# The fullest expert taken first, its first two thirds beside the last block's routing

## The chip, the cores and the metric

The kernel runs on one core of a Trainium2 chip. The metric is the device time of one execution in microseconds (us): the median of three runs, and beside it one execution taken with the hardware profiler.

## The reference

One transformer layer over 4096 tokens of width 256, on one sequence. Attention has 16 heads of width 16, LoRA terms on its three projections, an ALiBi bias and a causal mask. A mixture of 8 experts follows, two per token, each expert with a capacity of 1076 rows. Both halves add their input and end in a layer norm.

```python
x = _layernorm(x + attention(x))           # softmax(q k / 4 + slope (i - j), causal) v, then Wp
probs = softmax(x @ Wg)                    # 8 experts
topv, topi = top_k(probs, 2); gates = topv / sum(topv)
pos = (place of the token among those of its expert, in order of tokens); keep = pos < 1076
dest = where(keep, expert * 1076 + pos, dropped)
h = gelu(expert_in @ W1[e] + b1[e])        # 256 -> 1024, each expert
y = h @ W2[e] + b2[e]                      # 1024 -> 256
x = _layernorm(x + sum over the two choices of y[dest] * gate * keep)
```

## The kernel before

The five engines (and SyncE, which issues most DMAs) each run a list of instructions written out by hand, with waits on semaphores; nothing reorders them. There are two blocks of code, with a barrier of all engines between them: `attend` and `experts`.

`attend` runs 411 turns. It takes the queries in 8 blocks of 512 and, beside the attention of later blocks, routes the earlier ones: `Router` multiplies a block's attention by Wp, normalizes it, chooses two experts per row (`choose`), counts rows per expert (`pe_count` on TensorE, `places` on VectorE), and GpSimd scatters the rows into `slots_x` in DRAM, 1076 rows for each expert. `PIECE_AT`, `SCATTER_AT` and similar tables say in which turn each piece runs. Blocks 0 to 6 are routed there; the last scatter of block 6 is in turn 379, and `FLAG_TURN` is 382.

The last block (7) can only be routed when all of attention is done, so that is the start of `experts`, in class `Last`. VectorE scales the attention rows (`scale_last`), TensorE multiplies them by Wp (L2083), VectorE normalizes and chooses (`vector`), TensorE counts (L1870), ScalarE applies the norm (L2198), GpSimd issues eight scatters (L2034). Meanwhile SyncE loads the fp32 weights of experts 0 and 1 and the constants (`Last.sync`), and TensorE runs 80 matmuls whose result nobody reads (`warm`, L2093). When the last scatter has landed, SyncE loads the rows of experts 0 and 1 (L2334 to L2336).

Each expert then has 9 tiles of 128 rows (the ninth has 52), in three groups `SB` of three tiles. TensorE transposes the tiles (`transpose`, L2398), runs 8 `up`s for each group (6 matmuls each, L2410), and a `down` for each tile (24 matmuls, L2429). Matmuls are done in three products of bf16 halves: a high half (cast) and a low half (the difference). ScalarE does the gelu (`hidden`, L2477), VectorE the two halves of its result (`split`, L2529 and L2531) and the output (`out`), ScalarE and GpSimd the two halves of the weights (`weights_high` L2257, `weights_low` L2263), and GpSimd adds the weighted rows to the result in DRAM (L2366). PSUM holds four results of `up` (`ps_h`), so `up` number q waits for the gelu of number q - 4. All experts compute all their 9 tiles, however full they are. `Combine` ends the kernel with the second layer norm.

A register is loaded from SBUF in one place before: `flag_of` (L883), by each engine in turn 382, followed by two register instructions and a jump over a path that isn't taken.

## Time and profile before

| | us |
|---|---|
| median of 3 runs | 1240.04 |
| lowest, highest | 1238.25, 1240.32 |
| the profiled execution, its own time | 1237.03 |
| its span, first to last instruction | 1235.0 |
| TensorE busy | 1157.4 |
| ScalarE busy | 904.3 |
| VectorE busy | 637.3 |
| GpSimd busy | 351.2 |

The profile gives the busy time of each engine, a timeline of instructions with what ended the idle time before them, and busy times by window. Attention fills the span to 781 us, the last block's routing goes to 819, the eight experts to 1199, and the last layer norm to the end. A row with "x8" is eight instructions, its time the stretch that they fill. SPq and ACTq are the issues of DMAs. PEld is TensorE's loading of weights, which overlaps its matmuls.

### The profile page before, as it was taken

Reading aid. Unit: us, or ns where it says so; the run is one execution under the profiler, and the core shown is the slowest. Engines: PE = TensorE matmul, PEld = TensorE weight load, DVE = VectorE, ACT = ScalarE, POOL = GpSimd, SP = SyncE. Lnnn points to the kernel's source line nnn. Section 1 sums busy time; section 2 is a strip of 40 time slices with the busy share of each in tenths; the row PEclk is TensorE's granted clock in tenths of the full one; section 3 lists DMA queues with packets and bytes.
Section 4 is the critical chain, followed back from the end, with each engine's and each line's share of the span. In section 5 each row is a group of like instructions: output and inputs, shape, how many; then the busy total and the mean of one; then the engine's idle time right before and its main releaser. Section 6 shows DMA issues by size and latency. Waiting matters only on the chain. (4 is left out here: it accounts for less than half of the span.)

```text
span 1235.0 us, 24778 instructions
## 1 busy us (share of the span) xinstructions
PE 1157.4 (94%) x8880; PEld 507.9 (41%) x8880; DVE 637.3 (52%) x1802; ACT 904.3 (73%) x1181; POOL 351.2 (28%) x391
## 2 busy tenths in 40 slices
PE   9999999999999999999999989699999999999980
PEld 4322222222222222222222111277777777787770
DVE  5644343132366335734353203548767767767747
ACT  3889999999998999999999989344434435535314
POOL 5421111101123112232122220033453453552440
PEclk9999999999999999999999999799999999999995
DMA  6743421322321331213120100543443523430226
GB/s 194 169 109 81 95 67 59 81 87 73 82 76 52 111 86 42 73 64 101 45 74 31 47 14 26 180 141 84 115 74 81 129 37 101 122 35 11 28 23 272
DMA packets 84100, 104.10 MB, mean 84 GB/s; under 512 B 15416, under 2 KB 69309, under 8 KB 83985
## 3 DMA queue, kind: packets, MB, share of 16 engines
q1 hardware_dynamic: 66520, 76.80, 22.0%
q0 software_dynamic: 15968, 24.12, 9.3%
q10 hardware_dynamic: 1496, 1.68, 0.5%
q8 instruction: 68, 1.11, 0.4%
q14 instruction: 48, 0.39, 0.1%
HBM read 56.88 MB, written 47.96 MB: 85 GB/s over the span
## 5 line engine op out<-in xcount | busy, mean ns | idle before, releaser
L1491 ACT ACTIVATE prob<-ps_s 128x1024 f32<-128x1024 f32 (+4 forms) x841 | 706.1, 999 | 46.6 <-PE ps_s L1380 44.7
L1397 PE MATMUL ps_o<-prob,v_aug 128*17 128x512 f32 (+3 forms) x3236 | 423.5, 570 | 3.5 <-DVE acc L1575 2.8
L1380 PE MATMUL ps_s<-qop,kop 51*128 51x512 f16 (+3 forms) x1618 | 260.4, 369 | 18.6 <-ACT prob L1491 7.2
L1380 PEld LDWEIGHTS ps_s<-qop,kop 51*128 51x128 f16 x1618 | 62.5, 93 | 386.1 <-ACT prob L1491 366.8
L2429 PE MATMUL ps_y<-w2s,hs 128*128 128x256 bf16 (+1 forms) x1728 | 189.1, 273 | 1.2 <-DVE yb L2515 1.2
L2410 PE MATMUL ps_h<-xs,w1s 128*128 128x384 bf16 (+1 forms) x1152 | 179.9, 316 | 5.2 <-ACT hid L2477 4.4
L2477 ACT ACTIVATE hid<-ps_h,b 128x384 f32<-128x384 f32 (+1 forms) x192 | 105.0, 559 | 108.7 <-PE ps_h L2410 83.7
L1575 DVE COPY acc<-ps_o 32x512 f32<-32x512 f32 (+2 forms) x108 | 74.2, 687 | 190.1 <-PE ps_o L1397 188.7
L2429 PEld LDWEIGHTS ps_y<-w2s,hs 128*128 128x128 bf16 (+1 forms) x1728 | 157.3, 98 | 18.6 <-DVE yb L2515 1.5
L2366 POOL DMA_INDIRECT result<-y,entry x72 | 111.6, 1550 | 176.4 <-DVE y L2520 141.6
L1527 POOL TENSOR_SCALAR_AFFINE_SELECT prob<-prob 128x256 f32<-128x256 f32 (+1 forms) x179 | 68.6, 394 | 310.8 <-ACT prob L1491 308.4
L2410 PEld LDWEIGHTS ps_h<-xs,w1s 128*128 128x128 bf16 x1152 | 111.0, 98 | 68.9 <-ACT hid L2477 7.1
L2034 POOL DMA_INDIRECT slots_x<-xsplit,dest_all x64 | 63.3, 989 | 253.0 <-ACT prob L1491 197.4
L2468 ACT ACTIVATE xs<-ps_x 128x512 bf16<-128x512 bf16 (+1 forms) x72 | 40.0, 569 | 105.4 <-PE ps_x L2398 105.3
L1397 PEld LDWEIGHTS ps_o<-prob,v_aug 128*17 128x17 f32 x3236 | 59.8, 95 | 136.0 <-issue 80.0
L2529 DVE CAST hs<-hid 128x384 bf16<-128x384 f32 (+1 forms) x192 | 91.9, 478 | 39.2 <-ACT hid L2477 38.7
L2531 DVE TENSOR_TENSOR hs<-hid,hs 128x384 bf16<-128x384 f32 (+1 forms) x192 | 102.2, 532 | 6.6
L2520 DVE TENSOR_SCALAR y<-yb,weight 128x256 f32<-128x256 f32 (+1 forms) x72 | 48.6, 676 | 13.0 <-DMA result<-y,entry 8.2
L829 DVE CAST x_all<-ps_r 128x256 f16<-128x256 f32 x24 | 10.2, 424 | 79.6 <-PE ps_r L680 79.6
L2515 DVE TENSOR_TENSOR yb<-ps_y,b 128x256 f32<-128x256 f32 x64 | 27.0, 422 | 41.5 <-PE ps_y L2429 41.2
L2263 POOL TENSOR_TENSOR w1s<-w,w1s 128x2048 bf16<-128x2048 f32 x7 | 28.5, 4078 | 45.3 <-ACT w1s L2257 26.5
L1901 DVE TENSOR_TENSOR slogit<-ps_r,xg 128x8 f32<-128x8 f32 x28 | 4.7, 167 | 71.0 <-PE ps_r L1865 70.9
(206 smaller groups left out, 795.0 us busy)
## 6 DMA issues: line engine op xcount, KB each, us to landing
w<-in_W SPq DMA_DIRECT2D x16, 1024.0 KB, 7.5
slots_x<-empty POOLq DMA_DIRECT2D x12, 520.0 KB, 3.8
qop<-fparts_q SPq DMA_DIRECT2D x42, 128.0 KB, 4.9
xe<-slots_x SPq DMA_DIRECT2D x8, 650.0 KB
aT<-attnT SPq DMA_DIRECT2D x16, 256.0 KB
x_all<-in_x SPq DMA_DIRECT2D x8, 512.0 KB
result<-x_all SPq DMA_DIRECT2D x8, 512.0 KB
x_all<-result SPq DMA_DIRECT2D x8, 512.0 KB, 6.6
```

Source lines behind the costliest of these rows:

```text
L1380: mm = pe.matmul(ps_s[:, u.p % SLOTS_S, e, a.q0:], o.key(e, a.h, a.kt), o.query(e, a.h, a.b, a.q0), start=True, stop=True)
L1397: mm = pe.matmul(ps_o[32 * c:32 * c + VW, a.q0:], o.v[:, a.kt, a.h], prob[:, t % RING, c % 2, c // 2, a.q0:], start=a.first, stop=a.last)
L1491: act.activation(prob[:, t % RING, n, e:z, q0:], ps_s[:, u.p % SLOTS_S, e:z, q0:], ACT.Exp, scale=1.0 / (SCALE * SCALE)).then_inc(exp_done, 1)
L1527: pool.affine_select(own, own, [[0, z - e], [1, P]], ALU.is_ge, 0.0, base=0, channel_multiplier=-1).then_inc(masked, 1)
L1575: dve.tensor_copy(acc[rows, a], ps_o[rows]).then_inc(evicted, 1)
L2034: pool.indirect_dma_start(out=r.slots_x, out_offset=bass.IndirectOffsetOnAxis(ap=r.dest_all[:, n, m:m + 1], axis=0), in_=r.xsplit[:, m // ...
L2366: pool.indirect_dma_start(out=result, out_offset=bass.IndirectOffsetOnAxis(ap=entry[0:n, u, k:k + 1], axis=0), in_=y[0:n, k % 3], in_offse ...
L2410: mm = pe.matmul(ps_h[:, q % 4, 0:w], w1s[:, u, i1, c, m * P:(m + 1) * P], xs[:, u, i2, c, a:a + w], start=(t == 0 and c == 0), stop=(t == ...
L2429: mm = pe.matmul(ps_y[to:to + n, (ST * u + k) % 2, 0:D], hs[:, (3 * u + sbk) % 2, i1, m, o:o + n], w2s[:, u, i2, m, :], start=(t == 0 and ...
L2477: act.activation(hid[:, q % 4, 0:w], ps_h[:, q % 4, 0:w], ACT.Gelu_apprx_tanh, bias=b1[:, e, q % HC:q % HC + 1]).then_inc(gelu, 1)
L2529: dve.tensor_copy(hs[:, sl, 0, q % HC, 0:w], hid[:, q % 4, 0:w]).then_inc(h_high, 1)
L2531: dve.tensor_tensor(hs[:, sl, 1, q % HC, 0:w], hid[:, q % 4, 0:w], hs[:, sl, 0, q % HC, 0:w], ALU.subtract).then_inc(h_low, 1)
```

## The change

The order of the experts is now worked out on the chip. In turn 384 TensorE adds up the rows counted in blocks 0 to 6 (`pe_order`), VectorE takes the expert with most and writes a table in which it and expert 0 have changed places (`dve_order`, 8 small instructions). `expert_at` reads an entry of it into a register of SyncE. In turn 386 SyncE reads entry 0 and loads that expert's weights, and the rows of its first 6 tiles, into `First` (memory of `x1_all` that is free by then). ScalarE loads the gelu's table at the end of `attend`.

In `experts` TensorE first transposes the 6 tiles, then runs the last block's products (`Last.products`) between the first 8 ups, the count after 10 ups, 2 downs after 12, and 4 more downs after 16. Then it waits for the last three tiles of that expert. The first 8 gelu results are halved by ScalarE (high) and GpSimd (low), the others by VectorE. GpSimd also makes the low halves of this expert's weights, all ahead of its eight scatters; ScalarE does the first 8 gelus ahead of `last.scalar`. SyncE reads all 8 entries of the table, then loads the constants expert by expert (24 DMAs with a register in the address, 11 static ones before) and the weights of the second expert. The 80 matmuls are gone. From the second expert on the code is as before, but for unrolled loads on SyncE that fetch the weights before waiting for the rows.

```diff
 FLAG_TURN = max(max(SCATTER_AT), BOUND_TURN) + 3
+ORDER_TURN = FLAG_TURN + 2
+assert ORDER_TURN >= COUNT_AT[NB - 2] + 2
+PIECE_AT[ORDER_TURN] = ("order",)
...
+                    if t == ORDER_TURN + 2:
+                        sp.wait_ge(j.v_mm, NB * KT)
+                        sp.wait_ge(j.ws_done, 1)
+                        sp.wait_ge(j.xs_done, NB - 2)
+                        for m in range(4):
+                            sp.wait_ge(j.stored[m], j.stores(m, NB))
+                        first.load(sp, io)
...
+                    if kind == "order":
+                        r.pe_order(pe, ps_r[:, 0:E])
...
+                act.activation(j.warm[:], j.o.v[0:1, 0, 0, DH:VW], ACT.Gelu_apprx_tanh)
...
+    def pe_order(r, pe, out):
+        pe.wait_ge(r.count_done, NB - 1)
+        pe.matmul(out, r.ones[:], r.run[:], start=True, stop=True).then_inc(r.c_mm, 1)
+    ORDER_STEPS = 8
...
+    def dve_order(r, dve, bank):
...
+        c.did(dve.tensor_copy(r.filled[:], bank))
+        c.wait()
+        c.did(dve.max(r.most[:], r.filled[:]))
...
+        c.did(dve.tensor_copy(r.order[:, 0:1], r.chief[:]))
+        c.end()
...
+    def expert_at(r, eng, p):
+        eng.wait_ge(r.step, (NB - 1) * r.STEPS + r.ORDER_STEPS)
+        return eng.value_load(r.order[0:1, p:p + 1], min_val=0, max_val=E - 1)
...
-    def sync(l, sp, x, io):
+    def products(l, pe, c, s, out):
         r = l.r
-        x.load_weights(sp, io, 0, 0)
-        x.load_constants(sp, io)
-        x.load_weights(sp, io, 1, 1)
-        r.store_base(sp, l.N)
-        sp.wait_ge(r.scattered, NB * KT * 2 * 16)
...
-    def tensor(l, pe, out, count, warm):
-        r, u = l.r, l.N % 2
-        for c in (1, 0):
-            for s in range(KT):
-                if c == 0 or s == 0:
-                    pe.wait_ge(r.scaled, l.BASE + (KT if c == 1 else KT + s + 1))
-                mm = pe.matmul(out[:, s, 0:D + E], r.aT[:, u, c, s * P:(s + 1) * P], r.wp[:, c, :], start=(c == 1), stop=(c == 0))
-                if c == 0:
-                    mm.then_inc(r.y_mm, 1)
-        r.pe_count(pe, l.N, count[:, 0:KT * E])
-        for m in range(2 * KT + 1):
-            if m >= 1:
-                pe.wait_ge(l.issued, m)
-            for _ in range(10 if m == 0 else 3 if m < 2 * KT else 9):
-                pe.matmul(warm[:, 0:QB // 2], r.aT[:, u, 0, 0:P], r.aT[:, u, 0, 0:QB // 2], start=True, stop=True)
+        pe.wait_ge(r.scaled, l.BASE + (KT if c == 1 else KT + s + 1))
+        mm = pe.matmul(out, r.aT[:, l.N % 2, c, s * P:(s + 1) * P], r.wp[:, c, :], start=(c == 1), stop=(c == 0))
+        if c == 0:
+            mm.then_inc(r.y_mm, 1)
...
-        dve.wait_ge(l.issued, 2 * KT + 1)
-        for k in range(2):
-            x.weights_low(dve, 0, 0, k)
...
-            pool.sem_inc(l.issued, 1)
-        pool.memset(l.done[:], 0.0).then_inc(l.issued, 1)
...
+class First:
...
+    TILES = SB[1][1]
+    POOLED = HC
...
+        f.w1 = mem.take([P, 2, HID], F32)
+        f.w2 = mem.take([P, HC, D], F32)
+        f.xe = mem.take([P, f.TILES, ROW], F32)
+        f.ident = mem.take([P, P], BF16)
...
+    def load(f, sp, io):
+        e = f.r.expert_at(sp, 0)
+        sp.dma_start(f.ident, io["ident_b"]).then_inc(f.x_loaded, 16)
+        sp.dma_start(f.w1, io["W1"][e].rearrange("(c p) h -> p c h", p=P)).then_inc(f.w_loaded, 16)
+        sp.dma_start(f.w2, io["W2"][e].rearrange("(c p) d -> p c d", p=P)).then_inc(f.w_loaded, 16)
+        sp.wait_ge(f.r.scattered, 16 * 2 * KT * (NB - 1))
+        sp.dma_start(f.xe, f.rows[e, 0:f.TILES * P].rearrange("(k p) d -> p k d", p=P)).then_inc(f.x_loaded, 16)
...
+    def load_constants(x, sp, io, p, e):
+        signal = x.const[min(p, 1)]
+        sp.dma_start(x.b1[:, p:p + 1], io["b1T"][:, bass.ds(e, 1)]).then_inc(signal, 16)
+        sp.dma_start(x.expert[:, p:p + 1], io["expert_no"][:, bass.ds(e, 1)]).then_inc(signal, 16)
+        sp.dma_start(x.b2[:, p], io["b2"][bass.ds(e, 1)].broadcast_to([P, D])).then_inc(signal, 16)
...
+        outs = [*(ps_x[:, i].bitcast(F32)[:, 0:D + E] for i in range(2)), *(ps_y[:, i, 0:D + E] for i in range(2))]
+        count = ps_x[:, 0].bitcast(F32)[:, 0:KT * E]
+        def turned(k):
+            return ps_h[:, k % 4].bitcast(BF16)[:, 0:4 * P].rearrange("p (c n) -> p c n", c=4)
...
-                last.sync(sp, X, io)
-                load(0, 0)
-                load(1, 1)
-                with sp.Fori(0, E // 2 - 1) as i:
-                    for u in range(2):
-                        e = 2 * i + u
-                        sp.wait_ge(ws, e * 2 + 2)
-                        sp.wait_ge(x_mm, e * ST + ST)
-                        sp.wait_ge(entry_done, e * 4 + 4)
-                        X.load_weights(sp, io, u, e + 2)
-                        load(u, e + 2)
+                    sp.dma_start(xe[:, u, 0:z], f.rows[e, 0:z * P].rearrange("(k p) d -> p k d", p=P)).then_inc(x_first[u], 16)
+                    sp.dma_start(xe[:, u, z:ST - 1], f.rows[e, z * P:(ST - 1) * P].rearrange("(k p) d -> p k d", p=P)
+                                 ).then_inc(x_loaded[u], 16)
+                    load_last(u, e)
+                order = [r.expert_at(sp, p) for p in range(E)]
+                X.load_constants(sp, io, 0, order[0])
+                X.load_weights(sp, io, 1, order[1])
+                for p in range(1, E):
+                    X.load_constants(sp, io, p, order[p])
+                r.store_base(sp, last.N)
+                sp.wait_ge(r.scattered, NB * KT * 2 * 16)
+                a = f.TILES
+                sp.dma_start(xe[:, 0, a:ST - 1], f.rows[order[0], a * P:(ST - 1) * P].rearrange("(k p) d -> p k d", p=P)
+                             ).then_inc(x_loaded[0], 16)
+                load_last(0, order[0])
+                load(1, order[1])
+                for p in range(2, E):
+                    e, u = p - 2, p % 2
+                    sp.wait_ge(ws, e * 2 + 4)
+                    X.load_weights(sp, io, u, order[p])
+                    sp.wait_ge(x_mm, e * ST + ST)
+                    sp.wait_ge(entry_done, e * 4 + 8)
+                    load(u, order[p])
...
+                def low(q):
+                    pool.wait_ge(h_high, q + 1)
+                    pool.tensor_tensor(hs[:, 0, 1, q, :], hid[:, q % 4, :], hs[:, 0, 0, q, :], ALU.subtract).then_inc(h_low, 1)
...
+                def first():
+                    for h in range(2):
+                        pool.wait_ge(X.wh, h + 1)
+                        to = (slice(None), 0, 1, slice(None), f.HALVES[h])
+                        pool.tensor_tensor(w1s[to], f.w1_part(h), w1s[:, 0, 0, :, f.HALVES[h]], ALU.subtract).then_inc(ws, 1)
+                    for q in range(f.POOLED):
+                        low(q)
+                        if q in (3, 6):
+                            w2_low(q // 4)
+                    last.gpsimd(pool)
+                    pool.wait_ge(r.base_stored, 16 * NB)
+                    for k in range(2):
+                        for t in range(*SB[k]):
+                            scatter(0, 0, t)
+                        X.weights_low(pool, 1, 1, k)
+                    for t in range(*SB[2]):
+                        scatter(0, 0, t)
+                first()
...
+                def first():
+                    pe.wait_ge(x_first[0], 32)
+                    for k in range(f.TILES):
+                        if k >= 4:
+                            pe.wait_ge(y_half, k - 3)
+                        rows = f.xe[:, k, 0:D].bitcast(BF16)
+                        for c in range(4):
+                            mm = pe.transpose(turned(k)[:, c], rows[:, c * P:(c + 1) * P], ident)
+                        mm.then_inc(x_mm, 1)
+                    for s in range(KT):
+                        last.products(pe, 1, s, outs[s])
+                    pe.wait_ge(y_half, 3)
+                    pe.wait_ge(x_out, 5 + 2)
+                    for m in range(HC):
+                        if m < 2:
+                            pe.wait_ge(ws, 1)
+                        if m == 1:
+                            pe.wait_ge(x_out, 5 + 3)
+                        if m == HC // 2:
+                            pe.wait_ge(ws, 2)
+                        up(0, 0, 0, m)
+                        if m % 2 == 0:
+                            last.products(pe, 0, m // 2, outs[m // 2])
+                    for m in range(2):
+                        up(0, 0, 1, m)
+                    pe.wait_ge(r.logits_out, last.BASE + KT)
+                    pe.wait_ge(r.summed, last.BASE + KT)
+                    r.pe_count(pe, last.N, count)
+                    for m in range(2, 4):
+                        up(0, 0, 1, m)
+                    pe.wait_ge(ws, 4)
+                    down(0, 0, 0, 0, False, [0, 1])
+                    for m in range(4, HC):
+                        up(0, 0, 1, m)
+                    down(0, 0, 0, 0, False, [2])
+                    down(0, 0, 0, 1, False)
+                    pe.wait_ge(r.placed, NB)
+                    pe.wait_ge(x_loaded[0], 32)
+                    for k in range(f.TILES, ST):
+                        transpose(0, 0, 0, k)
+                    pe.wait_ge(x_out, ST + 2)
+                    for m in range(HC):
+                        up(0, 0, 2, m)
+                        transpose(1, 0, 1, m)
+                    transpose(1, 0, 1, HC)
+                    down(0, 0, 0, 2, False)
+                first()
...
+                def first():
+                    act.wait_ge(f.w_loaded, 32)
+                    w1_high(0)
+                    for k in range(3, 5):
+                        rows_out(k)
+                    w1_high(1)
+                    rows_out(5)
+                    act.wait_ge(X.const[0], X.FIRST_CONSTANTS)
+                    for q in range(f.POOLED):
+                        hidden(0, q)
+                        act.wait_ge(gelu, 4 + q + 1)
+                        act.activation(hs[:, 0, 0, q, :], hid[:, q % 4, :], ACT.Identity).then_inc(h_high, 1)
+                        if q in (1, 3):
+                            w2_high(q // 2)
+                    last.scalar(act)
+                    for q in range(f.POOLED, 2 * HC):
+                        hidden(0, q)
+                    act.wait_ge(X.const[1], X.CONSTANTS)
+                    for k in range(2):
+                        X.weights_high(act, 1, 0, 1, k)
+                    for k in range(f.TILES, ST):
+                        tokens(0, 0, k)
+                    for m in range(HC):
+                        hidden(0, 2 * HC + m)
+                        tokens(1, 1, m)
+                    tokens(1, 1, HC)
...
+                def first():
+                    for k in range(3):
+                        dve.wait_ge(x_mm, k + 1)
+                        dve.tensor_copy(xs_of(0, k, P), turned(k)).then_inc(y_half, 1)
+                    last.vector(dve, outs, count)
+                    first_entries()
+                    dve.wait_ge(h_low, 4 + f.POOLED)
+                    for q in range(f.POOLED, 2 * HC):
+                        split(0, 0, q)
+                        if q < f.POOLED + 2:
+                            out(0, 0, q - f.POOLED)
+                    for k in range(2, f.TILES):
+                        out(0, 0, k)
+                    entries(0, 0, 0)
+                    for q in range(2 * HC, 3 * HC):
+                        split(0, 0, q)
+                    for k in range(f.TILES, ST):
+                        out(0, 0, k)
+                first()
```

SyncE, from the start of `experts` to the rows of the first expert. `w`, `b`, `expert_no` and `ident` are the weights, the biases, the experts' numbers and the identity. Before:

```order
L2249 DMA w<-in_W 128x2x1024
L2250 DMA w<-in_W 128x8x256
L2242 DMA ident<-in_ident_b 128x128
L2243 DMA b<-in_b1T 128x64
L2244 DMA expert_no<-in_expert_no 128x72
L2246 DMA b<-in_b 128x256 x8
L2249 DMA w<-in_W 128x2x1024
L2250 DMA w<-in_W 128x8x256
L2049 DMA result<-x_all 128x4x256 [waits x1_done]
L2334 DMA xe<-slots_x 128x3x260 [waits scattered]
```

Now, with "..." for the seven other loads of the table and for the constants of six more experts:

```order
L1929 TENSOR_LOAD order [waits r_step]
L1929 ISA x2
...
L2309 ISA
L2309 DMA b<-in_b1T 128x8
L2310 ISA
L2310 DMA expert_no<-in_expert_no 128x9
L2311 ISA
L2311 DMA b<-in_b 128x256
L2317 ISA
L2317 DMA w<-in_W 128x2x1024
...
L2425 ISA [waits scattered]
L2425 DMA xe<-slots_x 128x2x260
```

The first bias now stands behind eight register loads, where weights and constants were issued at once.

TensorE, at the start of `experts`. `aT` is the last block's attention, `xs` the transposed rows, `hs` the halved gelu results. Before:

```order
L2083 MATMUL ps_h<-wp,aT 128x264 [waits scaled]
L1870 MATMUL ps_y<-counts,before 128x32 [waits count_done]
L2093 MATMUL ps_y<-aT 128x256 x10
L2398 MATMUL ps_x<-ident,xe 128x128 [waits x_out,e_const,xe_first0]
L2410 MATMUL ps_h<-xs,w1s 128x384 [waits gelu,x_out,w_split]
```

Now, with "..." where ups and products go on in the same way:

```order
L2566 MATMUL ps_h<-x_all 128x128 [waits f_x_loaded]
L2129 MATMUL ps_x<-wp,aT 128x264 [waits scaled] x2
L2523 MATMUL ps_h<-xs,w1s 128x384 [waits w_split,gelu,x_out,y_half]
L2129 MATMUL ps_x<-wp,aT 128x264 [waits scaled]
...
L2523 MATMUL ps_h<-xs,w1s 128x384 [waits gelu,w_split]
L2523 MATMUL ps_h<-xs,w1s 128x384 x5
L2129 MATMUL ps_y<-wp,aT 128x264 [waits scaled]
...
L1894 MATMUL ps_x<-counts,before 128x32 [waits count_done,summed,logits_out]
...
L2542 MATMUL ps_y<-w2s,hs 128x256 [waits h_low,y_sum,w_split]
...
L2511 MATMUL ps_x<-x_all,xe 128x128 [waits x_out,placed,xe_loaded0]
```

The third and fourth product now stand behind the fifth and seventh up, which wait for gelus.

GpSimd, at the start of `experts`. Before:

```order
L2034 DMA slots_x<-xsplit,dest_all 8704x260 [waits split_low,gates,dest_done,tags]
L2034 DMA slots_x<-xsplit,dest_all 8704x260 [waits split_low] x7
L2216 MEMSET last_done 1x1
L2263 TENSOR_TENSOR w1s<-w,w1s 128x2048 [waits base_stored,w_high]
```

Now:

```order
L2482 TENSOR_TENSOR w1s<-x_all,w1s 128x2x512 [waits w_high] x2
L2471 TENSOR_TENSOR hs<-hid,hs 128x384 [waits h_high] x4
L2476 TENSOR_TENSOR w2s<-x_all,w2s 128x1024 [waits w_high]
L2471 TENSOR_TENSOR hs<-hid,hs 128x384 [waits h_high] x3
L2476 TENSOR_TENSOR w2s<-x_all,w2s 128x1024 [waits w_high]
L2471 TENSOR_TENSOR hs<-hid,hs 128x384 [waits h_high]
L2092 DMA slots_x<-xsplit,dest_all 8704x260 [waits split_low,gates,dest_done,tags]
L2092 DMA slots_x<-xsplit,dest_all 8704x260 [waits split_low] x7
```

Twelve subtractions now stand ahead of the eight scatters.

## Rows read from the trace of the kernel before

**Rows 1.** The page: busy time of each engine.

```profile
PE 1157.4 (94%) x8880; PEld 507.9 (41%) x8880; DVE 637.3 (52%) x1802; ACT 904.3 (73%) x1181; POOL 351.2 (28%) x391
```

**Rows 2.** Timeline, all engines, 782 to 822: start, us, engine, line, operation, tile.

```profile
782.53 0.53 SPq L1814 DMA_DIRECT2D aT<-acc  x1
...
783.20 0.54 SPq L1815 DMA_DIRECT2D total<-acc  x1
...
784.45 4.53 PE L2083 MATMUL ps_h<-wp,aT 128*128 128x264 f32 x12 [3.27 <-PEq L1284]
...
784.79 0.41 SPq L2249 DMA_DIRECT2D w<-in_W  x1
...
785.04 0.01 DVE L1827 LOAD_MASK_SELECT den<-total  x1 [3.13 <-DMA total<-acc]
...
798.93 0.60 ACT L2198 ACTIVATE x_all<-x_all,last_nmr,rstd 128x256 f32<-128x256 f32 x1 [2.15 <-DVE last_nmr L2106]
...
799.70 19.88 PE L2093 MATMUL ps_y<-aT 128*128 128x256 f32 x80
...
802.91 0.99 POOL L2034 DMA_INDIRECT slots_x<-xsplit,dest_all  x1 [51.38 <-DVE xsplit L2185]
...
811.92 0.98 POOL L2034 DMA_INDIRECT slots_x<-xsplit,dest_all  x1 [0.30 <-issue]
...
814.28 0.37 SPq L2334 DMA_DIRECT2D xe<-slots_x  x1
...
819.41 0.61 PE L2398 MATMUL ps_x<-ident,xe 128*128 128x128 bf16 x8
...
821.70 1.14 PE L2410 MATMUL ps_h<-xs,w1s 128*128 128x384 bf16 x6 [0.73 <-issue]
```

**Rows 3.** Busy time in windows of 2 us; the last three columns: granted clock, DMA.

```profile
core 0: us, PE busy (x) PEld busy (x) DVE busy (x) ACT busy (x) POOL busy (x), PEclk, DMA share, GB/s
...
796.00:798.00 2.00, 0.00 (x0) 0.00 (x0) 1.97 (x24) 0.78 (x1) 0.00 (x0) 0.50 1.05 407
...
806.00:808.00 2.00, 2.00 (x11) 1.74 (x11) 0.00 (x0) 0.00 (x0) 1.46 (x2) 1.00 0.10 32
```

**Rows 4.** Timeline, TensorE, first expert, to the first up of the second.

```profile
828.96 7.97 PE L2410 MATMUL ps_h<-xs,w1s 128*128 128x384 bf16 x48
...
839.58 2.78 PE L2429 MATMUL ps_y<-w2s,hs 128*128 128x256 bf16 x24
...
847.89 6.44 PE L2410 MATMUL ps_h<-xs,w1s 128*128 128x308 bf16 x48
...
869.43 1.50 PE L2429 MATMUL ps_y<-w2s,hs 128*52 128x256 bf16 x24
...
870.86 13.82 PE L2410 MATMUL ps_h<-xs,w1s 128*128 128x384 bf16 x84
```

**Rows 5.** Busy time in one later expert, the same columns as rows 3.

```profile
917.94:965.18 47.24, 46.53 (x398) 35.82 (x397) 34.02 (x76) 21.28 (x35) 22.01 (x12) 1.00 0.42 93
```

**Rows 6.** Timeline, TensorE, where it reads the flag into a register (turn 382).

```profile
732.17 0.61 PE L1380 MATMUL ps_s<-qop,kop 51*128 51x512 f16 x4 [3.48 <-issue]
```

**Rows 7.** Timeline, GpSimd and VectorE, where both work on SBUF.

```profile
679.96 1.04 POOL L2019 CAST xsplit<-x_all 128x1024 bf16<-128x1024 f32 x1 [7.73 <-DVE x_all L1911]
...
680.02 1.02 DVE L1937 TENSOR_TENSOR clogit<-slogit,shiftl 128x32 f32<-128x32 f32 x1
...
831.75 4.08 POOL L2263 TENSOR_TENSOR w1s<-w,w1s 128x2048 bf16<-128x2048 f32 x1 [18.78 <-issue]
...
832.08 3.97 DVE L2529 CAST hs<-hid 128x384 bf16<-128x384 f32 x1 [1.55 <-ACT hid L2477]
```

**Rows 8.** Timeline, ScalarE: a cast of w1, the table load, and a gelu.

```profile
793.07 1.91 ACT L2257 ACTIVATE w1s<-w 128x2048 bf16<-128x2048 f32 x1 [14.42 <-DMA w<-in_W]
...
803.22 1.28 ACT L2460 ACT_TABLE_LOAD   x1
...
824.17 0.58 ACT L2477 ACTIVATE hid<-ps_h,b 128x384 f32<-128x384 f32 x1
```

206 lines of the change are left out of this document (119 added, 87 removed).

## The prediction

> **What bounds the kernel now.** I read the page first: TensorE is busy for 1157 of 1235 us [rows 1], so the kernel is TensorE's list of work plus the places where it waits. The windows show that the experts are pure TensorE work: 46.53 us busy in the 47.24 us of one expert, at the full clock [rows 5]. Then I read the timeline of the one long place where TensorE does nothing useful, between attention and the first expert. Attention's last DMA is issued at 783.20, TensorE starts the last block's products at 784.45, ScalarE applies the norm from 798.93, GpSimd scatters from 802.91 to 812.9, SyncE loads rows from 814.28, the first transpose is at 819.41 and the first up at 821.70 [rows 2]. From 799.70 the engine is kept busy for 19.88 us by matmuls that nobody reads. So there are 37 us between attention and the first up, of which the products need about 7. The second expert starts at 870.86 [rows 4]; all after that is unchanged work. I therefore forecast when the second expert starts, and call the difference from 870.86 the gain.
>
> **What is moved out of the experts.** The first expert's 16 ups cost 1.0 us each (7.97 for eight) and its downs 2.62 (24 matmuls in 2.78, and the next starts while the last drains) [rows 4]. 16 x 1.0 + 6 x 2.62 = 31.7 us of TensorE work go into the 37 us. The whole could vanish if nothing in there waited: that is the upper bound of the gain, 31.7. The rest of this part is about why less comes.
>
> **Step 1, the first gelu.** ScalarE's first gelu waits for a bias that SyncE issues behind eight register loads. SyncE's first issue is at 784.79 now [rows 2]. The trace shows such a load in one place only: TensorE's stop in turn 382, 3.48 us with one load, two register instructions and a jump over a long piece of code [rows 6]. So one load is between 0 and 3.48. SyncE's way through the end of attention, two jumps and a barrier, is 1.05 us (783.20 + 0.54 to 784.79) [rows 2]; if the jump in turn 382 costs as much, 2.4 are left for the load. I take the middle between 0 and 2.4, 1.2, so eight cost 9.6 us. Two more issues at 0.67 (SyncE's issues with a register in the address, 782.53 and 783.20 [rows 2]) and 1.84 for landing (issue at 783.20, first use at 785.04 [rows 2]) give 784.79 + 9.6 + 1.3 + 1.84 = 797.6. The Trainium skill, page DMA: Bandwidth & Descriptors, section Latency and other measured facts, gives a floor of about 600 ns for a `tensor_load`; by it eight would cost 4.8 us and the first gelu would come at 792.8. The Trainium skill, page Runtime: NRT & Kernel Launch, section Instruction fetch mechanics, says that a taken branch to code outside the fetched window stalls on a fetch, which would put most of the 3.48 us on the jump. No run here separates the two yet.
>
> TensorE meanwhile does 6 transposes and 4 products of the first half (about 5.3), 4 ups and 2 products (4.8), so from 784.5 to 794.6, and then waits for a free bank of `ps_h`, that is for the first gelu. So here the loads are on the path for about 3 us of TensorE's own time, and for all of it on ScalarE's.
>
> **Step 2, ScalarE and GpSimd.** Eight gelus and eight casts of 384 columns: 0.58 for a gelu [rows 8], 0.42 for a cast (1.91 for 2048 columns [rows 8], scaled, with some fixed part) and 0.1 for the signal between them, 8 x 1.1 = 8.8. Two casts of half of w2 at 1.0: ScalarE is through at 797.6 + 10.8 = 808.4. GpSimd needs 4.08 us for 2048 columns [rows 7], so 0.77 for each of 8 lows and 2.04 for each of two halves, 10.2 in all, one step behind ScalarE: 809 if nobody is in the way. VectorE is. A VectorE instruction on SBUF waits for a GpSimd instruction on SBUF to end: a cast took 3.97 us beside a GpSimd subtraction of 4.08, and an addition of 32 columns took 1.02 beside a GpSimd cast of 1.04 [rows 7]. The norm and the choice of the last block, small instructions of which VectorE ran 24 between 796 and 798 [rows 3] and some 45 in all, fall in this very stretch, since the fourth product now stands behind the seventh up. Each must get in between two of GpSimd's. I add 5 us for the alternation (bounds: 0, and 10, where each of them would wait a quarter of a low); the eighth low is then done at 814.
>
> **Step 3, the downs.** TensorE's first down waits for that eighth low. Two downs 5.2, four ups 3.8, four downs 10.5: 814 + 19.5 = 833.5. The gelus of ups 12 to 15 need ScalarE to be done with `last.scalar`, which costs what it did (4.3 us from 798.93) plus a change of table in and out, since the gate needs exp: 2 x 1.28 [rows 8]. Norm at about 809.5, last gelu table at 816.5: under the two downs, so not on the path.
>
> **Step 4, the last three tiles.** GpSimd's eight scatters take 10.0 us as before (802.91 to 812.90), the wait to SyncE's issue 1.4 and the landing with transposes ready about 4 [rows 2]. They start when the lows are done and the rows are split, about 816, so the tiles are there at 816 + 10 + 1.4 + 4 = 831.4, under the downs. Transposes and copies of three tiles 2.3 (819.41 to 821.70 [rows 2]). Eight narrow ups 0.80 each (6.44 for eight [rows 4]), each with the transposes of a tile at 0.3 (two tiles in 0.61 [rows 2]): 8.8. Then the last halves from VectorE, which may stand beside GpSimd's 4.08 us on the second expert's w2: between 0 and 4, I take 2.5. Three downs 2.62 + 2.62 + 1.43 (869.43 to 870.86): 6.7. Sum 833.5 + 2.3 + 8.8 + 2.5 + 6.7 = 853.8.
>
> **Step 5, the clock.** The 80 idle matmuls are gone. The granted clock was at 0.50 from 796 to 798, with TensorE idle, and full from 806, after TensorE had been kept busy from 799.70 [rows 3]. Now TensorE waits from 794.6 to about 798 and runs with gaps after it, so some of the ups 4 to 9 run at the lower of the two levels (1.2 GHz) and take 1.92 instead of 0.96. Two or three such ups ahead of the fourth product delay it: 2 us, with bounds 0 and 6. Second expert at 855.8.
>
> **What costs nothing.** In attention TensorE gets one matmul of 8 columns and VectorE 8 small instructions, at some 24 in 2 us [rows 3]; ScalarE's exps are what attention waits for, and they wait for neither of these. SyncE's load and four issues in turn 386 are covered by 4 buffers of results; without this cover a turn is late by up to 3.48. The 2.8 MB that they move fall where the DMA engines are almost idle. The table of ScalarE at the end of attention lies under VectorE's last copies. The second expert's weights (2 MB) now start after the first constants and land by 808, needed at about 822. The 24 small constants end near 811, ahead of the gelus that need them. From the second expert on the lists are the same. The swap of experts by itself changes no time: each computes 9 tiles.
>
> **Sum.** 870.9 - 855.8 = 15.1 us less. Against the profiled execution's own 1237.0 that is 1221.9; the median of the runs shown lies 3.0 above that execution, so I forecast 1240.0 - 15.1 = 1224.9.
>
> **The rivals.**
> - *Register loads are nearly free and the engines hardly meet.* For: nothing in rows 6 says that the load and not the jump takes the time, and GpSimd's lows are short. Loads at 0.3 take 7.2 off; then the products, not the bias, set the start, and without the 5 us of step 2 and half of the other waits the second expert starts at about 845. The floor by TensorE's work alone is 784.5 + 38 (transposes 3.3, products 3.8, ups and downs 31) + 17.3 = 840. Gain 26: 1214. Chance 0.16. With the 600 ns that the Trainium skill's page on DMA gives, alone, the time would be 1220.1.
> - *The moved work mostly comes back as waiting.* Loads at 2.4 (the bound above) add 9.6, so the second expert starts at 865.4 and the gain is 5.5: 1234.5. With 5 more from GpSimd and VectorE it is 1239, within 0.2% of no change. Chance 0.16 for a small gain and 0.07 for none.
> - *Slower: each register load costs the whole stop.* If the jump in turn 382 is free (for it: TensorE's loop jump in the experts shows no gap) and a load costs 3.48, eight cost 27.8, 18.2 more than assumed: the second expert starts at 874.0, 3.1 late: 1243.1; with 5 us more of step 2 1248. The gain turns into a loss from 1.2 + 15.1 / 8 = 3.1 us a load. Against it: a load is one word from SBUF, and a whole DMA with its landing takes 1.84. Chance 0.06.
>
> **How the numbers follow.** Forecast case, loads of 0.5 to 1.9 us and a gain of 10 to 21: chance 0.55. The range reaches to the fast rival's 1214 and, above, into the small gains, to 1237. A measurement of this kernel can tell about 0.2% (2.5 us) from no change. Faster by more 0.55 + 0.16 + 0.16 = 0.87, within it 0.07, slower 0.06.
>
> **What would show it.** Step 1: time between the barrier and SyncE's first DMA, about 10 us, divided by eight; the first gelu near 797.6, with TensorE waiting for ScalarE before its fifth up. Step 2: VectorE's small instructions stretched to 0.3 to 0.8 us, GpSimd's eighth low near 814, the first down right behind it. Step 3: no wait for ScalarE after the second down. Step 4: the last transposes wait for nothing from DMA. Step 5: a window at 0.50 between 796 and 804. The forecast is wrong if the constants come before 792 or after 805, if the scatters start much later than 816 and the last tiles become the path, or if the barrier after attention moves from 784.

## The result and the profile after

| | before | after |
|---|---|---|
| median, us | 1239.14 (6 runs) | 1247.28 (6 runs) |
| lowest, highest | 1235.3, 1240.32 | 1244.69, 1250.76 |
| the profiled execution | 1237.03 | 1247.83 |
| its span | 1235.0 | 1245.6 |

The ratio is 1.0073, with a 95% interval of 1.0056 to 1.0091: slower by 8.1 us (by the medians), where 15.1 us less were forecast. The page of the changed kernel, its busy times and the granted clock in 40 slices; TensorE has 10 us less work in it than in [rows 1] (the 80 idle matmuls are gone) and yet the span is 10.6 us longer:

```profile
PE 1147.3 (92%) x8801; PEld 493.4 (40%) x8801; DVE 629.5 (51%) x1800; ACT 908.2 (73%) x1190; POOL 367.3 (29%) x402
...
PEclk9999999999999999999999989989999989999995
```

A slice is 31.1 us. The first dip of the clock is the stop of turn 382 ([rows 6]); the other two lie at 810 to 841 us, in the first expert, and at 996 to 1028, among the later ones, which ran at the full clock before [rows 5]. The timeline of the changed kernel, all engines, from the barrier to the second expert, answers [rows 2] and [rows 4]:

```profile
786.82 0.54 SPq L1839 DMA_DIRECT2D total<-acc  x1
...
788.07 2.46 PE L2566 MATMUL ps_h<-x_all 128*128 128x128 bf16 x24 [3.26 <-PEq L1289]
...
793.31 0.35 SPq L2309 DMA_DIRECT2D b<-in_b1T  x1
...
794.37 0.70 SPq L2311 DMA_DIRECT2D b<-in_b  x1
...
798.81 0.58 ACT L2624 ACTIVATE hid<-ps_h,b 128x384 f32<-128x384 f32 x1 [6.58 <-DMA b<-in_b]
...
809.73 2.03 DVE L1688 TENSOR_TENSOR tmp<-tmp 128x4 f32<-128x4 f32 x1
...
811.71 0.90 POOL L2471 TENSOR_TENSOR hs<-hid,hs 128x384 bf16<-128x384 f32 x1
...
815.19 0.18 PE L1894 MATMUL ps_x<-counts,before 128*128 128x32 bf16 x1 [7.58 <-DVE ahead L2181]
...
815.25 4.00 PE L2523 MATMUL ps_h<-xs,w1s 128*128 128x384 bf16 x12
...
819.04 5.44 PE L2542 MATMUL ps_y<-w2s,hs 128*128 128x256 bf16 x48
...
831.59 0.42 DVE L2696 TENSOR_TENSOR yb<-ps_y,b 128x256 f32<-128x256 f32 x1 [6.33 <-remote]
...
831.78 1.05 ACT L2624 ACTIVATE hid<-ps_h,b 128x384 f32<-128x384 f32 x2 [8.82 <-remote]
...
837.98 10.45 PE L2542 MATMUL ps_y<-w2s,hs 128*128 128x256 bf16 x72 [4.18 <-DVE hs L2712]
...
848.27 0.61 PE L2511 MATMUL ps_x<-x_all,xe 128*128 128x128 bf16 x8
...
861.91 6.83 PE L2542 MATMUL ps_y<-w2s,hs 128*128 128x256 bf16 x72 [2.06 <-DVE hs L2712]
...
868.67 3.59 PE L2523 MATMUL ps_h<-xs,w1s 128*128 128x384 bf16 x21
```

The second expert starts at 868.67 and not at 855.8. That is still 2.2 us earlier than before [rows 4]. So the loss lies behind it. TensorE's first up of four of the later experts in the changed kernel, then its last downs; the same last row of the kernel before stands in the fence after it:

```profile
915.76 1.47 PE L2523 MATMUL ps_h<-xs,w1s 128*128 128x384 bf16 x8
...
965.69 1.48 PE L2523 MATMUL ps_h<-xs,w1s 128*128 128x384 bf16 x8
...
1020.28 3.89 PE L2523 MATMUL ps_h<-xs,w1s 128*128 128x384 bf16 x12 [5.27 <-issue]
...
1069.28 0.99 PE L2523 MATMUL ps_h<-xs,w1s 128*128 128x384 bf16 x5
...
1195.32 14.69 PE L2542 MATMUL ps_y<-w2s,hs 128*128 128x256 bf16 x144
```

```profile
1189.82 9.45 PE L2429 MATMUL ps_y<-w2s,hs 128*128 128x256 bf16 x96
```

An expert took 47.24 us before [rows 5]. Now the second takes 47.1, the third 49.9, the fourth 54.6, the fifth 49.0, the sixth 49.2. From the first up of the second expert to the end of the last down it was 1199.27 - 870.86 = 328.4 us and is 1210.01 - 868.67 = 341.3.

The sum by stages, from the two profiled executions:

| stage | before | after | difference | forecast |
|---|---|---|---|---|
| to attention's first product with v | 30.89 | 33.23 | +2.3 | 0 |
| from there to the barrier | 753.6 | 754.8 | +1.3 | 0 |
| barrier to the second expert | 86.4 | 80.6 | -5.8 | -15.1 |
| second expert to the last down | 328.4 | 341.3 | +12.9 | 0 |
| the rest of the span | 35.7 | 35.6 | -0.1 | 0 |

The first line is no effect of the change: over all profiled executions of this study that first product lies between 30.4 and 33.9, for either kernel. The second stands at the stop of turn 382, 3.66 us here and 3.48 in [rows 6], behind which two turns and not one ran slowly; in the other executions of kernels with this attention the stage took 752.0 to 755.7. The two together, 3.6 us, lie within what these executions differ by. So the questions are the 12.9 and the 9.3 that are missing from the gap.

### The profile page after: what moved, and what is told of

It is laid out like the page before. It is cut to its first block and busy times, and to the rows that moved or that the text cites. A ratio compares the mean times of both kernels' runs of the same rounds, so it can differ in the third digit from the quotient of the medians.

```text
span 1245.6 us, 24718 instructions
## 1 busy us (share of the span) xinstructions
PE 1147.3 (92%) x8801; PEld 493.4 (40%) x8801; DVE 629.5 (51%) x1800; ACT 908.2 (73%) x1190; POOL 367.3 (29%) x402
## 5 line engine op out<-in xcount | busy, mean ns | idle before, releaser
L2523 PE MATMUL ps_h<-xs,w1s 128*128 128x384 bf16 (+1 forms) x1152 | 186.2, 319 | 18.5 <-ACT hid L2624 12.2
L2712 DVE TENSOR_TENSOR hs<-hid,hs 128x384 bf16<-128x384 f32 (+1 forms) x184 | 109.1, 593 | 6.3
L2617 ACT ACTIVATE xs<-ps_x 128x512 bf16<-128x512 bf16 (+1 forms) x66 | 36.5, 569 | 86.8 <-PE ps_x L2511 86.8
L2710 DVE CAST hs<-hid 128x384 bf16<-128x384 f32 (+1 forms) x184 | 78.5, 427 | 34.0 <-ACT hid L2624 33.6
L2701 DVE TENSOR_SCALAR y<-yb,weight 128x256 f32<-128x256 f32 (+1 forms) x72 | 41.2, 573 | 32.3 <-DMA result<-y,entry 27.7
L834 DVE CAST x_all<-ps_r 128x256 f16<-128x256 f32 x24 | 10.2, 425 | 79.7 <-PE ps_r L685 79.7
L685 PE MATMUL ps_r<-xs_half,ws_half 128*128 128x256 f16 x288 | 39.8, 274 | 0.0
```

The source lines that it names most:

```text
L2523: mm = pe.matmul(ps_h[:, q % 4, 0:w], w1s[:, u, i1, c, m * P:(m + 1) * P], xs[:, u, i2, c, a:a + w], start=(t == 0 and c == 0), stop=(t == ...
L2710: dve.tensor_copy(hs[:, sl, 0, q % HC, 0:w], hid[:, q % 4, 0:w]).then_inc(h_high, 1)
L2712: dve.tensor_tensor(hs[:, sl, 1, q % HC, 0:w], hid[:, q % 4, 0:w], hs[:, sl, 0, q % HC, 0:w], ALU.subtract).then_inc(h_low, 1)
```

## The experiments

Kernels of one set ran on one chip; the sets are e1 to e4, e5 to e8, e9 to e12, e13 and e14, e15 to e18, and each set had another chip. That turned out to matter (see e13). Times are medians; before took 1239.1, 1239.7, 1238.5, 1237.9 and 1237.1 us beside the five sets.

### The weight loads of the experts: e1 and e3

In the diff, SyncE's `load_weights` stands ahead of the waits for `x_mm` and `entry_done`. In the trace 2 MB each are issued at 908.96, 958.90, 1008.09 and 1062.49, which is 6.8 to 12.2 us before TensorE begins an expert; in the kernel before they were issued 2.8 to 3.7 us behind that. The changed kernel, timeline ahead of the fifth expert's start; GpSimd's `DMA_INDIRECT` is an add of 128 rows into `result`:

```profile
1008.09 0.37 SPq L2317 DMA_DIRECT2D w<-in_W  x1
...
1008.56 0.42 SPq L2318 DMA_DIRECT2D w<-in_W  x1
...
1011.81 1.55 POOL L2456 DMA_INDIRECT result<-y,entry  x1 [0.30 <-issue]
...
1016.49 0.35 DVE L2701 TENSOR_SCALAR y<-yb,weight 128x256 f32<-128x256 f32 x1 [5.49 <-DMA result<-y,entry]
```

VectorE may not overwrite `y` before the add into `result` that reads it has landed. It waits 5.5 us for that, here and, for 5.25 to 5.49 us, at the start of the third, fourth and sixth expert. In these three the first split comes 5.6 to 6.1 us behind TensorE's first up and not 2.8 to 3.2, and ScalarE's gelus and TensorE's ups stop behind the splits. e1 puts the loads back:

```diff
                     sp.wait_ge(ws, e * 2 + 4)
-                    X.load_weights(sp, io, u, order[p])
                     sp.wait_ge(x_mm, e * ST + ST)
                     sp.wait_ge(entry_done, e * 4 + 8)
+                    X.load_weights(sp, io, u, order[p])
                     load(u, order[p])
```

> The changed kernel with one thing undone: in SyncE's list of the experts the 2 MB of weights of expert e+2 are issued behind the waits for the transposes and the row numbers of expert e, as in the kernel before, and not ahead of them. Theory A (the early weight loads collide with the adds into result and with what the engines fetch at the start of an expert): the experts that took 49.9, 54.6, 49.0 and 49.2 us come back to 47.2, and 10 to 13 us of the whole time go: 1247 becomes 1234 to 1237. Rival B (the experts are late because of the lists themselves, the unrolled SyncE list or the GpSimd order): the periods stay and the time stays within 2 us of 1247. Rival C (only the stop of 5.3 us at the fourth expert comes from the collision): 1241 to 1243.

Measured: 1237.03 us, ratio to before 0.9995 (0.998 to 1.001). That is 10.2 us less than the changed kernel, each taken against the kernel before beside it. In the profiled executions the stretch from the second expert to the last down falls from 341.3 to 332.8 us, so theory A holds for 8.5 of the 12.9 there; the other 4.4 are the loop's (e9). e3 makes the opposite edit in the kernel before:

```diff
                         sp.wait_ge(ws, e * 2 + 2)
+                        X.load_weights(sp, io, u, e + 2)
                         sp.wait_ge(x_mm, e * ST + ST)
                         sp.wait_ge(entry_done, e * 4 + 4)
-                        X.load_weights(sp, io, u, e + 2)
```

> The kernel before with one thing changed: SyncE issues the weights of expert e+2 ahead of its waits for the transposes and the row numbers of expert e. Theory A (collision): from the third expert on the periods grow from 47.2 to 49 or more, one of them by over 5 us where the loop jumps, and the kernel takes 8 to 13 us more than before: 1247 to 1252. Rival B: 1239, no change.

Measured: 1249.79 us, ratio 1.0100 (1.0076 to 1.0124). So this one line, alone, costs the kernel before 10.7 us. On the chip of the last set the changed kernel and e1's ran again (e15, e16): 11.5 us apart. The row of the list of waits for VectorE's wait in question (total, times, longest), of the kernel before, the changed kernel, e1 and e3, in this order:

```profile
DVE y L2520 <- DMA result<-y,entry: 8.2, 8, 1.7
```

```profile
DVE y L2701 <- DMA result<-y,entry: 27.7, 11, 5.5
```

```profile
DVE y L2701 <- DMA result<-y,entry: 7.8, 6, 2.5
```

```profile
DVE y L2520 <- DMA result<-y,entry: 31.1, 12, 5.6
```

In e3 the periods are 48.3 to 50.5 us, but none is 54: where TensorE's loop jumps back (its fifth expert) it makes no stop. In e1 that period is still 50.0, with a stop of 2.69 us, and the next is 48.9. That is what e9 is about.

### The constants of the first expert: e2

e2 has e1's edit too. The three loads go to places of their own in attention; their readers, changed to match, are left out here.

```diff
+        sp.dma_start(f.b1, io["b1T"][:, bass.ds(e, 1)]).then_inc(f.r.const, 16)
+        sp.dma_start(f.expert, io["expert_no"][:, bass.ds(e, 1)]).then_inc(f.r.const, 16)
+        sp.dma_start(f.b2[:, 0], io["b2"][bass.ds(e, 1)].broadcast_to([P, D])).then_inc(f.r.const, 16)
         sp.wait_ge(f.r.scattered, 16 * 2 * KT * (NB - 1))
...
                 order = [r.expert_at(sp, p) for p in range(E)]
-                X.load_constants(sp, io, 0, order[0])
```

> As the run before, and b1, b2 and the number of the first expert are loaded in attention too, right behind its weights, so that the first gelu waits for no register load of SyncE after the barrier. Theory (the first gelu, at 10.7 us behind the barrier, holds back ups, gelus, lows and with them the norm and the choice of the last block): the first gelu comes some 5 us earlier, TensorE waits less at its fifth up, the count of the last block and the second expert come 3 to 5 us earlier than in the run before. Rival (VectorE's and GpSimd's work on the way to the count is what binds, not the gelu): under 1 us.

Measured: 1230.84 us, 6.2 less than e1, ratio to before 0.9944 (0.9922 to 0.9966). ScalarE in e2, where the barrier lies at 788.1:

```profile
794.20 0.58 ACT L2629 ACTIVATE hid<-ps_h,x_all 128x384 f32<-128x384 f32 x1 [2.02 <-issue]
```

The first gelu is 6.1 us behind the barrier (10.7 in the changed kernel), and TensorE's first down 27.0 (31.0). The profiled executions alone don't show the gain: from the barrier to the second expert e1 takes 79.9 us and e2 79.5. Part of it is lost again there: before the fourth down TensorE waits 4.0 us for VectorE's halves, where it waited 1.7 in e1, and the 72 matmuls behind that wait take 10.8 us and not 8.0. Also, e2's six times fall into 1229.5 to 1231.1 and 1236.1 to 1236.2 us, and its profile is of the upper group. On the chip of the last set the two kernels were run again (e16, e17): 5.3 us apart, and 3.4 in that stage. So the constants were on the path, for some 3 to 6 us.

### The stop at 825 us: e4 to e8, e11, e13, e14

Between 822 and 831 in the changed kernel ScalarE and VectorE stand without a cause that the profile knows ("remote"), while TensorE, which by its rows had done what VectorE awaits at 824.5 and what ScalarE awaits (up 12) about 1 us later, goes in steps of four matmuls.

e4 is e1's kernel with VectorE's outputs of the first two tiles moved behind its splits:

```diff
                     for q in range(f.POOLED, 2 * HC):
                         split(0, 0, q)
-                        if q < f.POOLED + 2:
-                            out(0, 0, q - f.POOLED)
-                    for k in range(2, f.TILES):
+                    for k in range(0, f.TILES):
                         out(0, 0, k)
```

> As e1_weights_late, and VectorE's outs of the first expert's first two tiles are done behind its splits of ups 8 to 15 and not between them. In the trace of the changed kernel VectorE stood 6.3 us at the out of the second tile and the fourth down then waited 4.2 us for the splits. Theory D (the order on VectorE makes the splits wait): the wait of 4.2 us before the fourth down goes, up to 4 us less than e1_weights_late. Rival E (TensorE, ScalarE and VectorE all stand still there for one common cause, between 825 and 831 us, whatever VectorE's order): the same time as e1_weights_late within 1 us.

Measured: 1238.99 us, 2.0 more than e1, and ScalarE stands 7.4 us. The order on VectorE is not the cause.

The next four are e2's kernel with one edit each. e5 leaves out six of the eight scatters:

```diff
             alone(pool)
-            r.scatter_rows(pool, n, m, r.scattered)
+            if m < 2:
+                r.scatter_rows(pool, n, m, r.scattered)
```

> As e2_const_early, and of the eight scatters of the last block's rows GpSimd issues only the first two; the other six are left out, so that most rows of the last block are missing from the experts' slots and the output is not the reference's. In the changed kernel and in e1 and e2 ScalarE stood exactly 8.8 us before its gelu of up 12, VectorE 4.9 to 6.3 us at the out of the second tile, and TensorE went in steps of four matmuls per 1.42 us, until about 1 us behind a run of nine indirect DMAs of GpSimd. Theory F (a run of back-to-back indirect DMAs of GpSimd holds up what TensorE signals to ScalarE and VectorE): the stops go or shrink to 1 to 2 us, and the second expert starts 6 to 8 us earlier. Rival G (the base store of 512 KB, or code that is fetched, causes them): ScalarE still stands 8.8 us there.

(SyncE's wait for the scatters is lowered by the six that are missing.) e6 takes `r.store_base(sp, last.N)` away and puts `sp.dma_start(result[(NB - 1) * QB:T], r.io["x"][(NB - 1) * QB:T])`, a store of the same size, behind the register loads:

> As e2_const_early, and the 512 KB store of the last block's base rows, which falls just ahead of the stop, is replaced by a copy of the same size from x at the head of SyncE's list of the experts (the residual of the last block is then not the normalized one, so the output is not the reference's). Theory F (the run of indirect DMAs): the stop of 8.8 us on ScalarE stays. Rival G (the base store): it goes.

e7 lets each scatter wait for the one before it:

```diff
             alone(pool)
+            pool.wait_ge(r.scattered, 16 * (n * 2 * KT + m))
             r.scatter_rows(pool, n, m, r.scattered)
```

> As e2_const_early, and each of the eight scatters of the last block waits for the one before it to have landed. The scatters then take some 2.6 us each instead of 1.3, so 21 us instead of 10, and the rows of the last three tiles come at about 837 instead of 827. Theory F (back-to-back issue): ScalarE's stop of 8.8 us gets under 3 us, TensorE's downs start 3 to 4 us earlier, and the whole is 0 to 5 us faster, since the last tiles come just in time. Rival: the stops last as long as the scatters do, and the second expert comes up to 10 us later.

e8 has ups 10 and 11 ahead of the last block's count:

```diff
-                    for m in range(2):
+                    for m in range(4):
                         up(0, 0, 1, m)
                     pe.wait_ge(r.logits_out, last.BASE + KT)
                     pe.wait_ge(r.summed, last.BASE + KT)
                     r.pe_count(pe, last.N, count)
-                    for m in range(2, 4):
-                        up(0, 0, 1, m)
```

> As e2_const_early, and on TensorE the ups 10 and 11 stand ahead of the last block's count, not behind it. TensorE stood 7.6 us before the count while their inputs were there. Theory (TensorE's list binds there): the two ups run in the gap and the first down starts 3 to 4 us earlier, right behind the count; the second expert comes 1 to 4 us earlier. Rival (VectorE and ScalarE, held up by the scatters, set the fourth down): no change, within 1 us.

Measured: e5 1225.27, e6 1223.99, e7 1237.23, e8 1224.95 us, and none of the four has the stop (ScalarE waits 2.6 to 2.9 us there, in e8 0.6). Four different edits that each cure it looked like a cause made of several parts, and e11 (e2 with the base store behind the scatters; 1228.66 us, no stop either) seemed to fit.

```diff
-                r.store_base(sp, last.N)
                 sp.wait_ge(r.scattered, NB * KT * 2 * 16)
+                r.store_base(sp, last.N)
```

> As e2_const_early, and SyncE issues the 512 KB store of the last block's base rows behind its wait for the scatters and not ahead of it. The stop of 8.8 us on ScalarE was there in e1 and e2 and gone in e5 (two scatters), e6 (no base store there), e7 (scatters one by one) and e8 (ups 10 and 11 ahead of the count). Theory H (the store and the run of scatters together cause it): with the store moved the stop is gone, and 4 to 6 us of e2's time go. Rival I (the store has nothing to do with it, the place of TensorE's work against the scatters has): the stop stays and so does the time.

But none of these sets had the unedited kernel in it. e13 is e2's kernel again, on a fourth chip:

> e2_const_early once more, unchanged. Its six runs fell into 1229.5 to 1231.1 and 1236.1 to 1236.2 us, and its profiled run, which shows the stop of 8.8 us on ScalarE, was of the upper group. If the stop comes in every execution of this kernel, the profile shows it again whatever its time. If it comes in some of them only, a profile near 1230 is without it and a profile near 1236 has it.

Measured: 1224.50 us, 6.3 less than the same kernel took in e2 (13.4 less than the kernel before beside it, e2 8.3). ScalarE in e2 and then in e13, the gelus of ups 8 to 11 and the one of up 12:

```profile
816.99 1.99 ACT L2629 ACTIVATE hid<-ps_h,x_all 128x384 f32<-128x384 f32 x4
...
827.77 1.05 ACT L2629 ACTIVATE hid<-ps_h,x_all 128x384 f32<-128x384 f32 x2 [8.79 <-PE ps_h L2528]
```

```profile
813.96 1.99 ACT L2629 ACTIVATE hid<-ps_h,x_all 128x384 f32<-128x384 f32 x4
...
818.73 0.58 ACT L2629 ACTIVATE hid<-ps_h,x_all 128x384 f32<-128x384 f32 x1 [2.78 <-PE ps_h L2528]
```

e14, beside e13, issues five of the eight scatters; with e13's result it can't answer its question any more:

```diff
-            r.scatter_rows(pool, n, m, r.scattered)
+            if m < 5:
+                r.scatter_rows(pool, n, m, r.scattered)
```

> As e2_const_early, and of the eight scatters of the last block GpSimd issues the first five; three are left out, so that rows are missing from the experts' slots and the output is not the reference's. In the changed kernel, e1 and e2 the stop ended 0.8 to 1.0 us behind the run of back-to-back indirect DMAs. Theory J (the stop lasts as long as the run): it is there and some 3.9 us shorter, about 5 us on ScalarE. Rival K (the stop needs the whole run or something near its end): it is gone, as in e5 with two scatters.

1225.58 us, no stop, like its unedited neighbour. The last set puts four kernels on one chip, one edit apart each:

> The changed kernel once more, unchanged, to be compared on one chip with the three that follow. e13 was the kernel of e2 and took 1224.5 us where e2 took 1230.8, and its profile is without the stop of 8.8 us. If the stop hangs on the chip or the session and not on the kernel, all four of this set have it or none has. Without it the changed kernel takes 6 to 10 us less than 1247: 1238 to 1241. With it 1245 to 1250.

> e1_weights_late once more, on the same chip as e15. The early weight loads cost 10 us there; 9 to 12 us less than e15 are expected, so 1228 to 1231 without the stop and 1236 to 1238 with it.

> The kernel of e2 and e13 on the same chip as e16. It brought TensorE's first down 4.1 us nearer to the barrier in e2 against e1. Expected: 3 to 5 us less than e16, so 1224 to 1226 without the stop. Rival (the difference between e1 and e2 was the stop in some executions only): under 1 us.

> The kernel of e8 on the same chip as e17. Its profile has 69.7 us from the barrier to the second expert, e13's has 68.7, so against the theory under which it was first tried, ups 10 and 11 ahead of the count gain nothing: within 1.5 us of e17. Rival: 3 us less, as was expected of e8.

| on one chip | us | ScalarE before the gelu of up 12 | barrier to second expert |
|---|---|---|---|
| e15, the changed kernel | 1248.19 | 8.59 | 79.0 |
| e16, as e1 | 1236.69 | 8.62 | 79.8 |
| e17, as e2 and e13 | 1231.36 | 8.54 | 76.5 |
| e18, as e8 | 1230.32 | 4.30 | 74.4 |

All four have the stop. In e18 it comes in pieces: ScalarE waits 4.30, 2.26 and 2.32 us before the gelus of ups 12, 13 and 14, 8.9 in all, where e8 had 2.1; e8 is the same kernel and had no stop. So it goes with the chip, or with something else that a whole set has in common, and not with anything that I edited: none of the ten profiled executions of sets 2 to 4 shows it, and all seven of the changed kernels in sets 1 and 5 do, as does the first profile of the changed kernel. What it is stays open. It is worth 5 to 8 us of the time, each kernel taken against the kernel before beside it (e2 and e17 against e13, e18 against e8), and the 76.5 us of e17 against the 68.7 of e13 from the barrier to the second expert (e2's profile, of its upper group, has 79.5). In e17, the clearest, TensorE's rows are these, with four matmuls or fewer between stops; the last of them starts with the release of VectorE (822.85) and ScalarE (823.04):

```profile
821.40 0.50 PE L2547 MATMUL ps_y<-w2s,hs 128*128 128x256 bf16 x3 [0.44 <-issue]
822.12 0.27 PE L2547 MATMUL ps_y<-w2s,hs 128*128 128x256 bf16 x1 [0.22 <-issue]
...
822.87 2.02 PE L2547 MATMUL ps_y<-w2s,hs 128*128 128x256 bf16 x17 [0.47 <-issue]
```

What e5 to e8 still say, against e13's kernel without the stop: two ups ahead of the count gain nothing (e18 against e17: 1.0 us; e8 has 69.6 us of gap, e13 68.7), since the first down comes 3.9 us earlier and the fourth then waits for VectorE's splits. Scatters that wait for each other cost 12 us against their neighbours: in e7 the last is issued at 834.02 and TensorE then stands for the rows:

```profile
840.66 1.01 PE L2517 MATMUL ps_x<-x_all,xe 128*128 128x128 bf16 x8 [9.69 <-issue]
```

### The jump and the clock: e9, e10, e12

All three are e8's kernel. e9 writes TensorE's loop out:

```diff
-                over_experts(pe, one)
+                for e in range(1, E):
+                    one(e, e // 2, e % 2, e < E - 1)
```

> As e8_ups_first, and TensorE's list of the experts has no loop: the seven later experts are written out one behind the other. In the changed kernel and all its variants TensorE stood 2.6 to 5.3 us at the head of the sixth expert that is worked on, where its loop jumps back, with nothing that it waited for, and the expert behind it took 1.7 us more at the lower clock; the kernel before jumps at the same place without a stop. Theory (the jump waits for its code): the stop goes, the periods are 47.2 throughout, and 4 to 5 us go. Rival (the stop hangs on where a piece of code begins and comes back elsewhere): the time stays within 1 us.

e10 puts 40 idle matmuls ahead of the count:

```diff
                     pe.wait_ge(r.summed, last.BASE + KT)
+                    for _ in range(40):
+                        pe.matmul(ps_y[:, 1, 0:D], w2s[:, 0, 0, 0, 0:P], w2s[:, 0, 0, 0, 0:D], start=True, stop=True)
                     r.pe_count(pe, last.N, count)
```

> As e8_ups_first, and TensorE runs 40 matmuls of 256 columns that nobody reads before the last block's count, where it stood 4.6 us and then ran the first 24 matmuls of the downs at the granted clock of 0.56 to 0.59. Theory (step 5: the lower level costs what the matmuls there take twice): the two downs take 5.3 us instead of 7.1, and the second expert comes up to 1.8 us earlier. Rival (the fourth down waits for the splits on VectorE anyhow): under 0.5 us.

e12 has both edits:

> e8_ups_first with the loop written out on TensorE and the 40 idle matmuls before the count, together. If both terms are real and add up, 1225 less 4.6 less 1.8: 1218 to 1220. If only one is, 1220 to 1223; if neither, 1225.

The expectation of e9 says sixth expert; it is the fifth in the order of work, the fourth of the written-out list. Measured on one chip: e9 1219.17 (ratio to before 0.985, 0.9829 to 0.9872), e10 1223.23, e12 1218.26 us (0.9851, 0.9825 to 0.9876). The loop is worth 5.0 us (e10 to e12; in the profiled executions 4.6, the 332.2 us of e8 from the second expert to the last down against 327.6 in e9), the idle matmuls 0.9 (e9 to e12), which these runs can't tell from nothing. TensorE at the start of its fifth expert in e8, and the same two stretches in e9 (the fourth and the fifth expert, 47.24 us each, full clock):

```profile
1000.81 15.50 PE L2528 MATMUL ps_h<-xs,w1s 128*128 128x384 bf16 x84 [2.91 <-issue]
```

```profile
946.89:994.14 47.25, 46.54 (x399) 35.84 (x397) 33.89 (x76) 21.27 (x35) 22.14 (x12) 1.00 0.41 91
994.14:1041.38 47.24, 46.54 (x399) 35.84 (x397) 34.18 (x76) 21.27 (x35) 21.98 (x12) 1.00 0.36 85
```

The traces also show why the kernel before jumps freely. The program's code arrives by DMA, in rows that the view of the queues calls "instruction". Queues in the kernel before from 1005 to 1108, which holds its jump (1012.42) and the two experts behind it, then e8 over a stretch of the same kind, 992 to 1098:

```profile
q1 hardware_dynamic: 4866, 6.43, 18.7%
q0 software_dynamic: 2910, 1.96, 17.4%
```

```profile
q1 hardware_dynamic: 4866, 6.43, 18.2%
q0 software_dynamic: 3029, 1.83, 15.9%
q8 instruction: 10, 0.16, 0.7%
```

The kernel before (and e3) loads no code there: its second pass through the loop needs none. Every changed kernel with the loop loads code there again, 16 KB at a time, and in all sixteen of their traces TensorE's first matmul behind the jump comes 1.8 us after one of these loads has ended (in e8 997.90 + 1.13, first matmul 1000.81). In the changed kernel that load begins 2.5 us after TensorE's last matmul, in e8 right at it, and that is the difference between stops of 5.27 and 2.91 us. Why the loop's code stays at hand in one program and not in the other, no run here shows.

The idle matmuls did what they should on the spot: in e10 the first two downs take 5.40 us against 7.07 in e8. TensorE's rows of e10:

```profile
805.86 4.53 PE L2592 MATMUL ps_y<-w2s 128*128 128x256 bf16 x40
...
810.67 5.40 PE L2547 MATMUL ps_y<-w2s,hs 128*128 128x256 bf16 x48
...
826.10 8.02 PE L2547 MATMUL ps_y<-w2s,hs 128*128 128x256 bf16 x72 [2.35 <-DVE hs L2717]
```

The 1.7 us come back as a longer wait of the fourth down for VectorE (2.35 against 1.73) and 0.99 before up 12. e9 and e12 are 1.5% below the kernel before beside them.

## Why the prediction was wrong

**What costs nothing: "From the second expert on the lists are the same."** This is the step that failed, and it decided the sign. SyncE's list is not the same: the weight loads passed two waits, and the sum put that at nothing without a reason. From the second expert to the last down the kernel takes 12.9 us more, and only 5.8 of the forecast 15.1 are gained ahead of it. e1 and e3 give the price of the moved loads from both sides, 10.2 and 10.7 us, e15 to e16 11.5. The loads are the same 2 MB in all of these; what mattered is that adds which VectorE waits for were on their way when they started.

**TensorE's loop**, a part of the same sentence: the jump back is free in the kernel before and costs 2.6 to 3.1 us of standing in every changed version with the loop and the late weight loads, and 5.2 to 5.3 with the early ones (the changed kernel and e15). In all but e2 and e18 the granted clock falls to about 0.5 as the expert behind the stop begins, and it takes 1.7 us more; with that the loop costs 5.0 us (e10 to e12). The rival of slow register loads used "TensorE's loop jump in the experts shows no gap" as an argument; that holds for the kernel before alone. The Trainium skill, page Runtime: NRT & Kernel Launch, section Instruction fetch mechanics, says that a taken branch outside the fetched window stalls on a fetch; by that the jump would have to be priced. The traces agree: where code is loaded at the jump, TensorE stands, and where none is loaded, it does not.

**Step 1**, the register loads. Size wrong, on the cheap side. SyncE leaves attention at 786.82 + 0.54, the way through the barrier takes 1.05 as before, and the first DMA is at 793.31: 4.9 us behind 788.41, so 0.61 for each of eight loads and not 1.2. The Trainium skill's floor of about 600 ns for a `tensor_load` (page DMA: Bandwidth & Descriptors, section Latency and other measured facts) would have given that sum, but the load itself takes only 0.26 to 0.46 us here, one follows the other after 0.55 to 0.81, and the rest is register instructions. The trace of the kernel before already had the row that separates the load from the jump in turn 382:

```profile
L883 PEldq TENSOR_LOAD <-flag x1: 488/488/488, 727.4 to 727.4; - x1
```

0.49 us (least, median and most are one value) of the 3.48, so most of that stop is not the load, and the rival of 3.48 a load could have been dropped. What I took too low is the landing: from the issue of the b2 row, spread over 128 partitions, to the gelu that waits for it are 4.4 us (794.37 to 798.81) and not 1.84. The first gelu is 10.7 us behind the barrier, forecast 13.1.

**Step 2.** Half right. VectorE's small instructions were stretched, to 2.03 us beside GpSimd's half of w2 (809.73), more than the 0.8 forecast. The eighth low is done at 812.6, 24.5 us behind the barrier (forecast 29.5). But the first down waited for something else: the stretched chain of the norm and the choice ends at 815.15, TensorE's count waits for it 7.58 us, and ups 10 and 11 stand behind the count. So the first down is 31.0 us behind the barrier, forecast 29.5: near, for another reason.

**Step 3.** Forecast 19.5 us for six downs and four ups, measured 29.2 (819.04 to 848.27). The stop at 825 us is most of it, the lower clock of step 5 some 2.4 us. In e13, without the stop and with the early constants, it is 68.7 us from the barrier to the second expert, where the forecast for the changed kernel was 71.3; with the 3.4 us (e16 to e17) to 4.0 (the first down) of the constants given back it would be about 72 to 73. So without the stop the forecast of the gap would have held to some 2 us; that is an estimate from kernels on several chips, since the changed kernel itself was not run on a chip without the stop.

**Step 4.** Right in its length: forecast 20.3 us with all its parts, measured 20.4 (848.27 to 868.67), with 2.06 us for the halves against 2.5. The scatters start at 818.5 and not 816; their rows were there in time.

**Step 5.** The mechanism was right, its size (2 us, bounds 0 and 6) about half: the lower clock came twice. Windows of the changed kernel, columns as in [rows 3]:

```profile
816.00:818.00 2.00, 2.00 (x8) 0.91 (x6) 1.54 (x9) 1.96 (x6) 0.00 (x0) 0.50 0.00 0
...
840.00:842.00 2.00, 2.00 (x12) 1.34 (x11) 0.00 (x0) 0.00 (x0) 2.00 (x2) 0.50 1.06 370
```

Ups 10 and 11 took 4.0 instead of 1.9 us and 72 matmuls of the downs 10.45 instead of the 8.02 that they take in e8: 4.5 us. It was not where I had put it (the windows from 792 to 812 are at 1.00), but behind TensorE's waits of 7.58 and 4.18 us.

**The rivals.** That the moved work mostly comes back as waiting is what the gap did (5.8 us gained, 5.5 in that rival), though not through slow register loads. (In the fast rival the floor's 17.3 us behind the downs should be 17.8 by the prediction's own parts, 2.3 + 8.8 + 6.7; nothing hangs on it.) The rival on the slow side had the right sign and the wrong mechanism. None of them held the later experts, and the range ended at 1237.

The idea of the change itself was not refuted: with the loads put back, the constants early, ups 10 and 11 ahead of the count and the loop written out (e9) it takes 1219 us, 19 less than the kernel before beside it, on a chip without the stop. On one with it that version was not tried.

## What to carry to other kernels

Read the diff of the engine that only issues DMAs with the same care as the others: a load that passes a wait is a change of its own, and it is priced by whose landing is awaited while it runs, not by how full the DMA engines are. Where a stretch of the program is said to be untouched, check its start times in every engine's list, and check where its loops jump.

Put the unedited kernel into every set of experiments, on the same chip. Five edits here "cured" a stop that was simply absent on their chip, and one run of the unedited kernel showed it.

## What was not expected of the hardware

- With two loads of 1 MB from DRAM issued while GpSimd's adds of 128 rows into DRAM are under way, VectorE waits up to 5.5 us for the landing of an add (changed kernel) or 5.6 (e3), and at most 1.7 in the kernel before.
- The jump back of TensorE's loop costs nothing where the trace shows no load of code around it (before, e3), and 2.6 to 3.1 us where 16 KB of code are loaded there, 5.2 to 5.3 beside the early weight loads; the first matmul comes 1.8 us after that load has ended. In fourteen of these sixteen traces the expert behind the stop starts at the lower clock (0.5 granted) and takes 1.7 us more than 47.24 where nothing else holds it up; in e2 and e18 the clock stays at 1.00 and it takes 47.25 and 47.24.
- In two of the five sets, and in the first profile of the changed kernel, ScalarE stands for 7.4 to 8.9 us, VectorE (but for e18) for 4.9 to 6.3, and TensorE goes in steps, in one place of these kernels, while eight indirect DMAs are issued one behind the other; in the other three they do not. The cause is open.
- A register load from SBUF took SyncE 0.26 to 0.46 us, and eight in a row with their register instructions 4.9; the gelu that waited for a DMA spreading one row over 128 partitions began 4.4 us after its issue.
